# Turning x on VectorE through DRAM in the expert stage, the last two FFN chunks by token halves, and VectorE's order in FFN block 0

## The reference

```
def _L0_xattn_ref(hidden_states, token_ids, Wg, Wu, Wd):
    ...
    for e in range(E):
        g = jax.nn.silu(jnp.einsum('bsd,fd->bsf', hidden_states, Wg[e]))
        u = jnp.einsum('bsd,fd->bsf', hidden_states, Wu[e])
        y = jnp.einsum('bsf,df->bsd', g * u, Wd[e])
        out = jnp.where((expert_ids == e)[..., None], y, out)
def _L0_ffn_ref(x, gate_w, up_w, down_w, gate_s, up_s, down_s):
    ...
    g = jnp.einsum('th,ih->ti', xf, gate_w) * gate_s
    u = jnp.einsum('th,ih->ti', xf, up_w) * up_s
    hdn = jax.nn.silu(g) * u
    out = jnp.einsum('ti,hi->th', hdn, down_w) * down_s
x = x + jnp.tanh(g_xattn[0]) * _L0_xattn_ref(_layernorm(x, axis=-1), itok_BxS_13_99985, ctx_2048, ctx_2048, ctx_2048)
x = x + jnp.tanh(g_ffn[0]) * _L0_ffn_ref(_layernorm(x, axis=-1), ...)
```

## Time and profile before

| | us |
|---|---|
| median of three runs | 390.19 (390.17 to 391.16) |
| profiled execution | 389.52 |
| its span, first to last instruction | 387.8 |
| TensorE busy in the span | 372.2 (96%) |
| VectorE busy | 243.2 (63%) |
| mean granted TensorE clock | 0.996 of full speed |

### The profile page before, as it was taken

The page is one execution under the profiler, slowest core; times in us unless marked ns, Lnnn a source line. Parts: engine busy times, 40 slices in busy tenths (PEclk is TensorE's granted clock), DMA queues, the critical chain, the costliest instruction groups (busy, mean ns, idle before and its releaser), DMA issues.

```text
span 387.8 us, 5577 instructions
## 1 busy us (share of the span) xinstructions
PE 372.2 (96%) x1741; PEld 302.0 (78%) x1741; DVE 243.2 (63%) x453; ACT 145.6 (38%) x263; POOL 85.9 (22%) x108
## 2 busy tenths in 40 slices
PE   3999999999999999999899999999999999999993
PEld 2477788888888878888788888888888888888882
DVE  6889856667877678877867256647335756322225
ACT  4366556565555444522332222332223232222230
POOL 7623443434352120021102101002201001200003
PEclk9999999999999999999999999999999999999998
DMA  6766666663221126242201222200132210100002
GB/s 221 263 248 229 210 227 243 217 209 109 82 75 60 56 88 213 70 148 81 70 13 54 108 85 92 69 27 27 81 135 78 85 27 27 72 9 0 0 0 112
DMA packets 21904, 40.89 MB, mean 105 GB/s; under 512 B 2672, under 2 KB 8816, under 8 KB 21888
## 3 DMA queue, kind: packets, MB, share of 16 engines
q1 hardware_dynamic: 17536, 26.50, 21.0%
q0 software_dynamic: 4352, 14.19, 9.8%
HBM read 28.36 MB, written 12.32 MB: 105 GB/s over the span
## 4 chain that ended last, share of the span: by engine, by line
PE 78%; DMA 7%; DVE 7%; POOL 3%; issue 3%; ACT 1%; SPq 0%; DVEq 0%; POOLq 0%
PE bank L1122 32%; PE bank L1018 25%; PE bank L1129 16%; PE bank L1004 2%; PE bank L1033 2%; DMA x_rows<-rows,sidx 2%; DMA rows<-dwT 2%; DMA ctx_in<-ctxT 2%; POOL rstd L392 2%; DVE sh L858 1%; DMA rows<-x_rows 1%; DMA rows<-x,gidx 1%; ACT hp L570 1%; DVE work L850 1%; DVE hp L863 1%
## 5 line engine op out<-in xcount | busy, mean ns | idle before, releaser
L1122 PE MATMUL bank<-work,wgu 128*128 (+1 forms) x720 | 167.4, 385 | 1.1 <-DVE sh L858 1.0
L1122 PEld LDWEIGHTS bank<-work,wgu 128*128 128x128 f32 x720 | 132.9, 188 | 29.0 <-DVE sh L858 1.5
L1018 PE MATMUL bank<-work,parts 128*128 (+1 forms) x432 | 110.6, 402 | 0.8 <-ACT parts L464 0.2
L1018 PEld LDWEIGHTS bank<-work,parts 128*128 128x128 f32 x432 | 78.5, 188 | 19.8 <-issue 2.9
L1129 PE MATMUL bank<-work,hp 128*128 128x512 f32 x352 | 87.1, 390 | 0.5 <-DVE hp L863 0.5
L1129 PEld LDWEIGHTS bank<-work,hp 128*128 128x128 f32 x352 | 65.9, 188 | 14.6 <-DVE hp L863 0.9
L858 DVE SCALAR_TENSOR_TENSOR sh<-bank,gs,sh 128x512 f32<-128x512 f32 (+1 forms) x45 | 33.2, 737 | 57.5 <-PE bank L1122 57.5
L570 ACT ACTIVATE hp<-sh 128x512 fp32r<-128x512 f32 (+1 forms) x45 | 28.0, 623 | 93.9 <-DVE sh L858 93.9
L564 ACT ACTIVATE sh<-bank,gs 128x512 f32<-128x512 f32 (+1 forms) x45 | 30.5, 677 | 70.6 <-PE bank L1122 67.5
L863 DVE TENSOR_TENSOR hp<-sh,hp 128x512 fp32r<-128x512 f32 (+1 forms) x45 | 30.6, 681 | 30.2 <-ACT hp L570 30.2
L392 POOL TENSOR_TENSOR rstd<-ve,half 128x1 f32<-128x1 f32 x31 | 21.7, 698 | 123.4 <-DVE ve L698 123.4
(11 more groups left out here) (128 smaller groups left out, 253.9 us busy)
## 6 DMA issues: line engine op xcount, KB each, us to landing
wraw<-guT SPq DMA_DIRECT2D x8, 704.0 KB
ctx_in<-ctxT SPq DMA_DIRECT2D x4, 1024.0 KB, 6.0
rows<-x_rows SPq DMA_DIRECT2D x8, 512.0 KB, 4.4
turned_rows<-xn SPq DMA_DIRECT2D x12, 256.0 KB, 2.2
rows<-turned_rows SPq DMA_DIRECT2D x12, 256.0 KB, 2.6
checked<-dwT SPq DMA_DIRECT2D x11, 256.0 KB
rows<-dwT SPq DMA_DIRECT2D x11, 256.0 KB, 2.7
rows<-x,gidx POOLq DMA_INDIRECT x19, 5.0
```

Of the source, the lines that this page charges most:

```text
L1018: mm = pe.matmul(out_ps[:, :], part(s)[:, c * P:(c + 1) * P], ctx_w(e, c, w), start=n == 0, stop=n == last)
L1122: mm = pe.matmul(out_ps[:, tiles.start * P:tiles.stop * P], wgu[:, row + h, w, c * P:(c + 1) * P], moving, start=n == 0, stop=n == last)
```

## The change

1. **x of tiles 6 to 18 is turned as in the FFN.** `norm(k+2)` now runs in step k, one step earlier; SyncE writes `xn` to DRAM and reads it back as quarter rows (`turn_rows`, 13 times more), VectorE transposes 32x32 blocks in step k+1 (`turn`), and `turned_hi` and `turned_lo` split the result from SBUF instead of PSUM. TensorE makes `turn_x` for tiles 0 to 5 only. Statistics run for tile k+3 at the end of step k, ahead of `update(k-1)` (before: tile k+2 in the middle). The turned columns come in another order (every fourth), so the experts' matrices are loaded with rows `(p c)` instead of `(c p)`, in pieces of 8 KB, and TensorE's own turns of x and h read every fourth column too.
2. **SyncE's queue** is rewritten: from row 3 on a weight row goes out in every second `turn_rows`, a check row in every one, and `load_rows(0)` in the fifth.
3. **The last two chunks of the last block** are made in token halves: tokens 0 to 255 of both chunks, the down products of tiles u = 0, 1 of the last three chunks, then tokens 256 to 511 and u = 2, 3. VectorE scales and adds u = 0, 1 between the halves.
4. **FFN block 0 on VectorE**: `weight_lo(c+1)` stands between the product and the low part of chunk c, where `weight_lo(c)` stood ahead of the product; in every block statistics stand ahead of the turn.

```diff
-    ctx_v = ctxT.rearrange("e (c p) f -> e p c f", p=P)
+    ctx_v = ctxT.rearrange("e (p c) f -> e p c f", c=KC)
...
+            for n in range(AHEAD):
+                turn_rows(n)
+                if n == 4:
+                    sp.wait_ge(S["ctx_lo"], EXPERTS * KC)
+                    sp.wait_ge(S["stored"], 16 * (BLOCK + EXPERTS - 1))
+                    load_rows(0)
+                if n % 2 == 0 and n < 10:
+                    weight_row(3 + n // 2)
+                if n + 4 < IC:
+                    check_row(n + 4)
...
                 if k + 4 < STEPS:
                     gather(k + 4)
+                if ON_PE - 1 <= k < STEPS - 3:
+                    inverse_std(k + 3)
...
+            def turn(n, expert):
+
+                dve.wait_ge(S["xq_in"], 16 * (n + 1))
+                dve.wait_ge(S["xlo_ready"], n + ON_PE)
+                dve.transpose(turned_x(expert).rearrange("p (h a g) -> p g h a", h=KC, g=QUADS),
+                              quarter_rows(expert).rearrange("p (g b h) -> p g h b", g=QUADS, h=KC))\
+                   .then_inc(S["xt_ready"], 1)
...
+            def step(k):
+                h_lo(k - 1)
+                if k + 2 < STEPS:
+                    norm(k + 2, ring_slot(k + 2))
+                if k + 1 > ON_PE:
+                    turn(k + 1 - ON_PE, True)
+                hidden(k)
+                if k + 1 == ON_PE:
+                    turn(0, True)
+                turned_lo(k + 1)
+                if k + 3 < STEPS:
+                    landed(k + 3)
+                    stats(k + 3, ring_slot(k + 3))
                 update(k - 1)
...
-            norm(18, ring_slot(18))
+            turn(18 - ON_PE, True)
...
-                    mm = pe.transpose(xt_ps[:, c * P:(c + 1) * P], xn[:, c * P:(c + 1) * P], ident[:, :])
+                    mm = pe.transpose(xt_ps[:, c * P:(c + 1) * P], every_fourth(xn, c), ident[:, :])
...
-                    mm = pe.transpose(ht_ps[:, c * P:(c + 1) * P], sh[:, c * P:(c + 1) * P], ident[:, :])
+                    mm = pe.transpose(ht_ps[:, c * P:(c + 1) * P], every_fourth(sh, c), ident[:, :])
...
                 first_product(k, e, ctx_ready)
-                turn_x(k + 1)
+                if turns:
+                    turn_x(k + 1)
                 second_product(k - 1, e=e_before)
...
+                end_half(0)
+                end_half(1)
                 pe.wait_ge(S["hlo_ready"], n)
-                pe.wait_ge(S["down_lo"], IC)
-                for u in range(BLOCK):
-                    down_tile(c - 1, u, passes)
-                    pe.wait_ge(S["hlo_ready"], n + 1 + u // 2)
-                    down_tile(c, u, passes)
+                for c in range(IC - 3, IC):
+                    pe.wait_ge(S["hlo_ready"], n + c - (IC - 3))
+                    for u in range(2):
+                        down_tile(c, u, passes)
+                end_half(2)
+                end_half(3)
```

236 lines of the change are left out of this document (137 added, 99 removed).

## The result

The changed kernel takes 397.74 us (median of 4 runs, 396.82 to 399.35), the kernel before 390.18 beside it. The ratio is 1.0203, with an interval of 1.0178 to 1.0229: it is slower, where 384.5 was forecast. The profiled execution of the changed kernel took 397.47 us and has a span of 395.7 us, 7.9 more than before.

The account below looks back on a forecast made before the run. TensorE's list was taken to bound nearly the whole span. Turns -5.7, dearer turns +0.7, stalls +1.5, block 0 -1.0, end -1.2 sum to -5.7 us: 383.8 profiled, 384.5 median; range 382.5 to 386.5, for 8 in 10 381.5 to 388.5.

Parts of the forecast that it names:

- TensorE's list: Expert stage: thirteen turns of x removed gain 5.7 us, dearer remaining turns cost 0.7; a step goes from 6.43 to 6.02.
- the prediction's own signs: Prediction is wrong if steps 6 to 9 exceed 6.2 us or stops between 9 and 16 exceed 4 us.
- rival C: Expert stage: path through DRAM paces ten steps at 7.4 us, time 397; sign: VectorE waits for quarter rows; chance 0.07.
- VectorE's price: Expert stage: 5.45 us of work fits a 6.02 step; steps 10 to 13 need 6.46; stall 0.2 us.
- The path through DRAM: Expert stage: write 2.2 plus read 2.6 us makes 4.8, 1.1 spare, so taken as 0.
- the gathers: Expert stage: gather loop of 10.35 us fits two steps; beside the load, with the `xn` write, 1.3 us stall once.
- Rival B: Expert stage: gathers pace it through slower scatters, 6.34 us a step, time 387.2; chance 0.13.
- The start: Kernel start with experts' matrices in 8 KB pieces: VectorE's splitting is what TensorE waits for; taken as 0, ends +0.5 and -0.5.
- Block 0: FFN block 0: TensorE's one stop of 1.04 us in chunk 8 goes, 1.0 us gained.
- The end: Last two chunks in token halves: VectorE ends at 383.0 instead of 384.21, 1.2 us gained.

Follow-up runs that it names:

- early_on_act: Changed kernel with weight rows 3 to 5 issued early from ScalarE's queue, the last two as halves in SyncE's steps 8 to 11, x1 in two steps: 387.71 us.
- loads_on_act: Changed kernel with weight rows, check rows and the first x1 issued from ScalarE's queue instead of SyncE's: 396.46 us, ratio 1.0176.
- spread_loads: Changed kernel with the same bytes, weight rows as halves in steps of their own, the two x1 loads two steps apart: 394.03 us, ratio 1.0103.
- stop_bare: Kernel before with ScalarE made late once, at tile 10, by six idle activations, so TensorE stops: 394.82 us, ratio 1.0135.
- clock_fill: Changed kernel with 9 and 12 idle matmuls on TensorE ahead of the turns of h(6) and h(10): 398.56 us, ratio 1.0205.
- layout_2kb: layout_alone with each expert's matrix loaded in four transfers with pieces of 2 KB instead of one with 8 KB: 392.25 us, ratio 1.0051.
- block0_alone: Kernel before with only VectorE's new order in the FFN blocks: 388.86 us, ratio 0.9968.
- tail_alone: Kernel before with only the last two chunks made by token halves: 390.11 us, ratio 1.0001.
- stop_filled: stop_bare with 11 idle matmuls on TensorE in the stop: 393.02 us, ratio 1.0083.
- layout_alone: Kernel before with turns of every fourth column and experts' matrices in pieces of 8 KB, x still turned on TensorE: 393.16 us, ratio 1.0077.

## Why the prediction was wrong

**TensorE's list** was right. A step is 5.97 us where 6.02 was forecast, and 13 of them with the last ones gave 6.0 us; forecast was 5.7 less 0.7 for the dearer turns. By the prediction's own signs the rest was wrong: steps 6 and 7 took 10.48 and 8.06 us, not under 6.2, and VectorE waited for the quarter rows, which is rival C's sign.

**VectorE's price** was right as work: it fits into the step. Steps 10 to 13, with block 0's statistics, take 6.07 to 6.48 us in early_on_act, where VectorE's list was put at 6.46. But these four are 1.4 us longer than four of 5.97, where the lag was to be taken up but for 0.2; VectorE is busy for 23.3 of the 26 us from 88 to 114 there. In the changed kernel the stops hid it, and the steps behind the third stop took 5.97.

**The path through DRAM** is the step that failed. I took 0 for it, on two sentences: that the path is 4.8 us with 1.1 to spare, and that weight and check rows "are through about when that write comes". They are issued 1.2 us before the next write (55.18 and 56.35), x1 2.9 us before it (81.44 and 84.36), and at the 322 GB/s of the busiest stretch 960 KB take 3.0 us and 1.98 MB 6.3: neither is through when the write comes. But this does not give the size either: with the head start taken off and the write's own 2.2 added it comes to 4.0 and 5.6 us, and the rows show 6.55 and 7.7. What fits is all the traffic from the loads' issue to the write's landing, first the second stop's, then the third's, and the 7.2 us write of loads_on_act:

```profile
55.18:62.90 7.72, 6.05 (x29) 4.98 (x28) 4.95 (x9) 3.64 (x9) 2.45 (x3) 1.00 0.74 231
81.44:92.03 10.59, 10.59 (x52) 8.86 (x51) 7.26 (x14) 6.52 (x13) 2.77 (x5) 1.00 0.86 292
```

```profile
83.98:95.39 11.41, 9.73 (x44) 7.75 (x44) 8.70 (x18) 4.51 (x10) 3.16 (x4) 1.00 0.80 271
```

Length times GB/s is 1.78, 3.09 and 3.09 million bytes. The loads, the write itself, and the gather, the scatter and the read of quarter rows issued around them (256 KB each; no scatter in the first) are 1.77, 3.08 and 3.08 million. So in these three cases the write landed about when everything on the way had moved, whoever had issued it, at 231 to 292 GB/s. The earlier trace rows had shown the like, one scatter 2.3 us later beside 1 MB, and I used this for the gathers and `xn` once, as 1.3 us. In its place stand 7.8 us, of which 1.67 are the first stop, with no load ahead of it.

loads_on_act, spread_loads and early_on_act show the cause from three sides: another queue, with one pair of loads behind its write by chance, gives 1.3 us, the same bytes in other steps 3.7, and early_on_act, with three of the weight rows ahead of the path and the rest spread, 10.0.

**Rival C** named this mechanism and nearly its time (397), but in ten steps of 7.4 us. It came as three stops, and other steps ran at 5.97; of the 12.8 us that these stops cost, 5.0 were half clock, which C did not have. So the mechanism of C is borne out, and the nearness of its time is luck. By the Trainium skill, DMA: Bandwidth & Descriptors, "Latency and other measured facts", an HBM access takes 0.2 us on average and 2 us at high load, and I gave that little weight. Here one write beside heavy loads took 4.4 us more than the median, another 5.5; the direction agrees, and the size, of a whole transfer and not of one access, is more than the page has.

**Rival B**, the gathers, is real too but hidden behind C: it shows once the loads are spread (GpSimd's round of 7.71 us), and gives way by 1.5 us to an earlier power.

**The half clock** (5.0 us) stood in no part of the forecast; each stop was priced at its own length. stop_bare shows that a stop of 3.1 us in this kernel costs 394.82 - 389.93 = 4.9 us. It does not follow every stop: matmuls at full clock followed one of 1.67 us in the changed kernel, one of 2.54 in loads_on_act (there the half clock came behind the next one, of 1.69) and one of 3.12 in clock_fill. What decides it no run shows.

**The start** was taken as 0 and cost 1.66: the second gather lands 7.3 us after its issue instead of 5.8 beside matrices that come in pieces of 8 KB, and VectorE's list, which I had held for the limit, waits for it. layout_2kb gives 1.1 us of it back (product 1 of tile 4 at 44.46 instead of 45.59).

**Block 0**: forecast -1.0, measured -1.24 in the changed kernel's trace and -1.2 by block0_alone's ratio. Right, and for the reason given: the power takes 0.55 to 0.57 us in all four chunks of the changed kernel's block 0, where it took 1.41 to 1.46 beside `weight_lo`.

**The end**: forecast -1.2. VectorE did end 0.9 sooner. It is 0.3 short because the last down tile before the adds was put at 0.45 us: its two matmuls start after a wait and take 0.75 to their end (0.76 in the changed kernel). The larger part is that I let the span end a fixed 3.3 us after the last scatter's issue, and it took 4.0 to 4.9 in the kernels with this order. The term is 0 in tail_alone. What delays the last packets is not settled.

## What to carry to other kernels

When work is moved to a path through DRAM, add up all the bytes that any queue issues around each of its transfers and divide by the rate that a busy stretch shows (231 to 292 GB/s here); an average share of the DMA engines says nothing of it. Move the large loads away from the path before judging the idea: with the same loads at other times it went from 2% slower to 0.6% faster, a third of a per cent of it from block 0 alone. And price a stop of TensorE of two or three us at its length plus something between nothing and as much again (0 to 2.9 us here), since the clock may fall with it.

## What the runs showed of the hardware

- After a stop of 3.14 us (stop_bare) TensorE ran at half clock for part of the next step (granted clock 0.57 over 4 us); with idle matmuls in the same stop (stop_filled) it did not. After stops between 1.7 and 3.2 us in the other kernels it fell at some (2.47 and 3.18 in the changed kernel, 2.22 in clock_fill) and not at others (1.67, 2.54 in loads_on_act, 3.12 in clock_fill).
- A write of 256 KB to DRAM took 2.2 us at the median before, 6.55 behind 960 KB issued just ahead of it in its queue, 7.7 behind 1.98 MB there, and 7.2 beside the same 1.98 MB in another queue (loads_on_act). The first one of the changed kernel took 4.0 with no load just ahead.
- A gather beside transfers with pieces of 8 KB landed in 7.5 us (layout_alone; 7.3 in the changed kernel, 5.8 before), with pieces of 2 KB in the same kernel (layout_2kb) in time for a start 1.1 us sooner.
- The power of one column on GpSimd took 1.41 to 1.46 us beside VectorE's `weight_lo` and 0.54 to 0.57 without it (block0_alone).
- From the last scatter's issue to the end of the span it was 3.2 to 3.3 us where four follow each other closely, and 4.0 to 4.9 in every kernel that splits the last two chunks.
